# Layer 2 of a graph network: loads of sorted groups one group further ahead, and two blocks of counts no longer stored

## What is computed

```
agg = segment_sum(h[src], dst) / max(cnt, 1)
h   = relu(agg @ W_l + b_l + h @ W_r)                 # twice; the second time is "layer 2"
x   = layernorm(x + h @ W_out + b_out)
...
out    = selu(concat(x[src], edge_attr) @ W1a + b1a) @ W1b + b1b
mean   = segment_sum(out, dst) / max(cnt, 1)
x      = layernorm(x + selu(concat(x, mean, u) @ W2a + b2a) @ W2b + b2b)
```

## Time and profile before

| what | us |
|---|---|
| median of 3 runs | 2593.54 |
| lowest and highest | 2592.89 to 2598.89 |
| the profiled execution | 2589.51 |
| its span in the trace | 2587.8 |
| PE busy | 2099.7 (81%) |
| POOL busy | 1827.1 (71%) |
| DVE busy | 1593.5 (62%) |
| ACT busy | 1000.1 (39%) |

### The profile page before, as it was taken

The page is one execution under the profiler, slowest core; times in us unless marked ns, Lnnn a source line. Parts: engine busy times, 40 slices in busy tenths (PEclk is TensorE's granted clock), DMA queues, the critical chain, the costliest instruction groups (busy, mean ns, idle before and its releaser), DMA issues. The chain is left out here.

```text
span 2587.8 us, 53172 instructions
## 1 busy us (share of the span) xinstructions
PE 2099.7 (81%) x18808; PEld 1547.7 (60%) x18808; DVE 1593.5 (62%) x3209; ACT 1000.1 (39%) x2287; POOL 1827.1 (71%) x1859
## 2 busy tenths in 40 slices
PE   1899999999999999955887788887788788766753
PEld 1555555555555555535766676676676666656653
DVE  6889999994545555454655656565566555543433
ACT  3777787772000000023433334333333333332322
POOL 5535767646777777767777777777777777777775
PEclk9999999998999999966989998889899989986665
DMA  8368778769767878724333333333333333332212
GB/s 295 107 227 247 211 234 259 197 226 251 237 183 222 244 236 243 172 75 118 79 67 77 76 72 69 77 74 74 68 77 69 72 75 76 70 64 55 51 40 45
DMA packets 501618, 350.13 MB, mean 135 GB/s; under 512 B 378596, under 2 KB 452767, under 8 KB 497693
## 3 DMA queue, kind: packets, MB, share of 16 engines
q1 hardware_dynamic: 385571, 274.97, 37.6%
q0 software_dynamic: 54240, 57.27, 10.3%
q10 hardware_dynamic: 61562, 14.60, 3.1%
HBM read 201.07 MB, written 145.49 MB: 134 GB/s over the span
## 5 line engine op out<-in xcount | busy, mean ns | idle before, releaser
L985 POOL DMA_INDIRECT A_sb<-source_terms,src_cur x1132 | 1082.5, 956 | 345.2 <-issue 340.6
L936 POOL DMA_INDIRECT sorted_edges<-pm_row,pm_to x480 | 523.0, 1090 | 178.8 <-issue 137.6
L1870 DVE TENSOR_TENSOR arena<-iota_code,arena 128x2048 f16<-128x2048 f16 (+1 forms) x392 | 438.4, 1186 | 27.5 <-PE cnt_ps L1415 25.4
L1080 ACT ACTIVATE A_sb<-cnt_ps 128x392 f32 (+1 forms) x784 | 383.8, 498 | 125.1 <-PE cnt_ps L1415 84.4
L1544 PE MATMUL agg_ps<-A_sb,arena 128*128 128x448 f16 x1911 | 382.3, 358 | 0.0
L1415 PEld LDWEIGHTS cnt_ps<-arena 128*128 128x128 f16 x3136 | 190.5, 101 | 214.9 <-issue 167.9
L1415 PE MATMUL cnt_ps<-arena 128*128 128x98 f16 x3136 | 281.4, 214 | 31.8 <-ACT A_sb L1080 26.6
L1646 PE MATMUL agg_ps<-A_sb 128*65 128x48 f32 x2264 | 188.6, 245 | 140.9 <-DVE A_sb L2206 140.9
L2193 DVE TENSOR_TENSOR cnt_ps<-cnt_ps,A_sb 128x512 f32<-128x512 f32 (+1 forms) x142 | 98.2, 692 | 315.1 <-DMA A_sb<-source_terms,src_cur 305.5
L1544 PEld LDWEIGHTS agg_ps<-A_sb,arena 128*128 128x128 bf16 x1911 | 187.2, 99 | 167.7 <-issue 9.9
L1228 ACT ACTIVATE A_sb<-cnt_ps 128x512 f32<-128x512 f32 (+1 forms) x142 | 84.3, 594 | 490.4 <-DVE cnt_ps L2193 477.6
(11 more groups left out here) (308 smaller groups left out, 3425.5 us busy)
## 6 DMA issues: line engine op xcount, KB each, us to landing
counts_matrix<-A_sb SPq DMA_DIRECT2D x14, 5488.0 KB, 17.0
A_sb<-counts_matrix SPq DMA_DIRECT2D x12, 5488.0 KB, 18.9
arena<-in_edge_attr_dram SPq DMA_DIRECT2D x93, 256.0 KB
sorted_edges<-zrow SPq DMA_DIRECT2D x12, 1716.0 KB, 12.0
arena<-sorted_edges SPq DMA_DIRECT2D x156, 128.0 KB
A_sb<-source_terms,src_cur POOLq DMA_INDIRECT x1132
overlapping_rows<-A_sb SPq DMA_DIRECT2D x1, 13056.0 KB, 39.4
A_sb<-in_edge_attr_dram SPq DMA_DIRECT2D x48, 256.0 KB
```

Source lines behind the costliest of these rows:

```text
L936: pool.indirect_dma_start(out=sorted_d, out_offset=bass.IndirectOffsetOnAxis(ap=pm_to[:, k, j:j + 1], axis=0), in_=pm_row[:, k, j, :], in_ ...
L985: pool.indirect_dma_start(out=gath[k][:, j * F:(j + 1) * F], out_offset=None, in_=p_d, in_offset=bass.IndirectOffsetOnAxis(ap=src_cur[k][: ...
L1080: act.activation(Asb(half)[:, :, bass.ds((b * BG + k) * GROUP, GROUP)].rearrange("p b (w j) -> p b w j", j=PAIR), cnt_ps[k % 2][:, 0:SUB * ...
L1870: ins = dve.tensor_tensor(hot_rows[:, slots], iota_code[:, 0:n, :].unsqueeze(1).to_broadcast([P, AT_ONCE * SUB // 2, n, 2]), turned[:, bas ...
```

## The change

Three edits.

In stage 1, blocks 12 and 13 of the counts are no longer stored: SP returns ahead of the wait and the store for them, the DRAM tensor has 12 blocks, and SP's wait for all stores counts one less for each half.

In layer 2, ACT issues the third load of a block in another place. `load_group(FIRST[s] + 5)` now stands behind `move_agg2(s)` in every block, where it stood only in four-group blocks. In a three-group block that is group FIRST[s + 1] + 2, and so the load of that group at the start of the next block is dropped. Behind a four-group block, and in block 1, the load at the start of the block stays. Eight loads move: groups 22, 29, 32, 39, 42, 49, 52 and 59.

```
-    A_d = dram("counts_matrix", [NSB, P, SRC_BLOCKS * SBN], FP16)
+    A_d = dram("counts_matrix", [NSB - 2, P, SRC_BLOCKS * SBN], FP16)
...
                     for q in range(s - 1, FROM_SP):
                         load_group(q)
+                if s >= NSB - 2:
+                    return
                 sp.wait_ge(counts_moved, (s + 1) * SB_GROUPS + 2)
...
-            sp.wait_ge(A_stored[0], 16 * PAIRS)
-            sp.wait_ge(A_stored[1], 16 * PAIRS)
+            sp.wait_ge(A_stored[0], 16 * (PAIRS - 1))
+            sp.wait_ge(A_stored[1], 16 * (PAIRS - 1))
...
                     act.activation(hTs[:, :], t_ps[:, 0:SBN], ACT.Copy).then_inc(hT_moved, 1)
-                if s is not None:
+                if s is not None and (s == 1 or LAYER2[s - 1] == 4):
                     load_group(FIRST[s] + 2)
...
                     load_group(FIRST[s] + 4)
                     move_agg2(s)
-                    if LAYER2[s] == 4:
-                        load_group(FIRST[s] + 5)
+                    load_group(FIRST[s] + 5)
```

## The result

| | before | after |
|---|---|---|
| median of 5 runs each, us | 2593.54 | 2576.11 |
| lowest to highest, us | 2590.45 to 2598.89 | 2574.71 to 2582.07 |
| profiled execution, us | 2589.5 | 2574.7 |
| its span, us | 2587.8 | 2573.0 |
| first to last copy of the sums of layer 2, us | 458.3 | 447.1 |

The changed kernel is 17.4 us faster, a ratio of 0.9932 [0.9919, 0.9944]. The forecast was 22.9 us. Between the two profiled executions it is 14.8 us: the gathers start 19.7 sooner, and the stage behind them is 4.9 longer.

What follows compares the result with a forecast made beforehand. The gathers were taken as a fixed-length block, with POOL becoming layer 2's bound. Gathers 20.9 us earlier plus 2 from the stores gave 22.9, so 2593.5 - 22.9, about 2571 us; range 2560 to 2585.

Steps and rivals of the forecast that it cites:

- Rivals 2: Layer 2: early load shares engines with the reload, landing about 716 instead of 719; gain 12 + 2, 2579 us; chance 0.14.
- Rival 1: Layer 2: POOL is no bound, its instructions get shorter, PE's whole side arrives: 29.5 + 2 to 5, 2560 us; chance 0.08.
- rival 3: Layer 2: transfer order makes no difference, or the group is late for its buffer; only the stores' gain left, 2591 us; chance 0.09.
- PE's 29.5 us: Layer 2: PE time lost in four four-group blocks, 7.9 us in one and 21.6 in the other three, stalls and half clock together.
- 20.9 + 2: Gathers start 20.9 us earlier from POOL ending layer 2 sooner, plus 2 us from dropping two stores; 22.9 in sum.
- prediction's own signs of being wrong: Wrong if POOL still waits for DVE, PE's shift ends below 20 us by new lower-clock stalls, or the last stage grows.
- Part 2: Layer 2: POOL becomes the bound, so PE's 29.5 us shrinks to 18.8 on POOL's side; gathers start 20.9 us earlier.
- 25.4 - 6.6 = 18.8 us: Layer 2: POOL's 22 waits for DVE total 25.4 us; less their usual 0.30 us steps, 18.8 can be taken out.
- the landing of 2.5 us: Layer 2: a scatter's buffer comes free 2.5 us after its last scatter ends, a figure taken from a gather.
- the 1.7 us of issues: Layer 2: after group 59's load finds its buffer free at 1072.2, ACT is free 1.7 us of issues later, at 1073.9.
- PE may run up to 23.2 ahead: End of layer 2: ACT's t_ps copy moves at most 19.1 us, plus 4.1 of PE slack; over 18.8, so POOL stays fed.
- rival 4: Layer 2: a moved load whose buffer is late blocks ACT's t_ps copy and PE at eight loads; 2608 us, slower; chance 0.05.

Runs made afterwards that it cites:

- the last run: Changed kernel with the last split of h moved from POOL to DVE and four-group blocks 1, 4, 7, 10: 2571.3 us, ratio 0.9912 to the kernel before.
- short reload: Changed kernel with each layer 2 reload bringing only the first seventh of a counts block: 2571.14 us, ratio 0.9887 to the kernel before.
- the second profile: Changed kernel run again, nothing altered, on the chip of the loads-only and stores-only runs: 2572.52 us, ratio 0.9942 to the kernel before.
- the kernel with the later load: Changed kernel with the remaining start-of-block loads issued behind the copy to h2T: 2580.9 us, ratio 0.992 to the kernel before.
- seven scatters of eight: Changed kernel with groups from 13 on scattered by seven indirect DMAs instead of eight: 2559.52 us, ratio 0.9845 to the kernel before.

## Why the prediction was right, and where it was off

**The mechanism was right.** Four of the eight loads were late behind the reload, and issuing them ahead of it took away DVE's four waits and PE's stalls with their half clock; with the old order and without the stores the waits stand as before (34.5 us). Against its block group 22's load moved by 5.8 us, and DVE had waited 8.20, so being earlier would by itself have left 2.4 us of wait. That the rest is the reload follows from this sum, and the last run points the same way: a load behind the reload, in a four-group block, was late by 7.13 us. No run has the old order with a short reload. Rivals 2 and 3 fall: group 22's destinations are there in time, and PE's scan wait is 0.6 us. Rival 1 falls as well: a scatter takes 985 ns in the mean, not less than 976. On one chip the loads alone bring 13 us where the whole change brings 15. Beside rival 3 the text had set a rule of the Trainium skill (DMA: Bandwidth & Descriptors, Queues, rings and completion order), by which the order of a small and a large transfer on two rows would hardly matter; here it mattered by 33 us of DVE's waits.

**That PE's 29.5 us would not all arrive was right**, and that the gathers would start about when POOL ends too. They start 19.7 us sooner against 20.9 + 2 forecast, but that this is so near is luck: POOL's run gave 10.9 of 18.8, and its start came 8.9 us earlier (630.4 instead of 639.2) where 2 were taken. The prediction's own signs of being wrong came in part: POOL still waits 4.5 us for DVE, PE's last copy moved by 19.8 us, under its 20, with new stalls that lower the clock, and the last stage of that profile grew.

**Part 2, POOL's share, was sized too large.** The step "only 25.4 - 6.6 = 18.8 us can be taken out" was taken as if all would be. 14.3 went, 4.5 stayed. The scatters themselves took 3.4 us more (367.0 to 370.4); a fixed 0.976 us each was the wrong assumption. POOL's run shrank by 10.9 us.

**The step that failed is the landing of 2.5 us, with the 1.7 us of issues behind it.** The landing was taken from a gather in the last stage, where no reload runs. Beside a reload a scatter's buffer comes free 7 to 14 us after its last instruction, as the lags of groups 36, 40, 46 and 49 show. The issues of one load were priced at 1.7 us; in block 10 they take 6.9 (968.42 to 975.33), and in block 7 of the second profile 12.0 (861.14 to 873.15), nearly all of it one stuck issue. "PE may run up to 23.2 ahead" rested on both. In fact PE met held loads in blocks 6 and 10, and they gave back 39.5 + 42.5 - 66.0 = 16 us. That is the mechanism of rival 4, at two blocks and not at eight loads, and one of the two was a load that had not moved (group 36, held at the copy to h2T). PE's side of layer 2 is 11.2 us shorter instead of 29.5. The iota shows it: forecast without a wait, it waits 2.15 us for PE's source terms.

**Part 3 was sized too small.** 2 us were taken, 6.0 [3.1, 8.8] measured, just outside the bound of 5, though the interval reaches inside it. PE's wait for the rows of x is gone, as forecast, but the half clock that follows it in the earlier trace rows was left out of the 2. The 20 us from just ahead of the same matmul (622.63 and 616.13), before and then in the changed kernel:

```profile
622.60:642.60 20.00, 19.97 (x93) 12.50 (x94) 4.07 (x13) 1.38 (x3) 10.71 (x12) 0.74 1.13 244
```

```profile
615.50:635.50 20.00, 19.33 (x106) 11.15 (x104) 5.40 (x19) 2.24 (x5) 13.86 (x15) 0.91 0.97 204
```

The granted clock is 0.91 instead of 0.74, which over 20 us is 20 x 0.17 = 3.4 us of full-speed work; with the wait of 1.70 that makes 5.1. POOL waits 2.60 us for ACT's h instead of 6.86. That these two make up the 6.0 is an estimate. This error and the one before it lean against each other, and the sum came out nearer than its terms.

**The last stage did not have the same length.** It differs between executions of the same code. In ten profiles of kernels with the same last stage a gather's mean is 956 or 957 ns in seven, with 1445.8 to 1447.5 us from the iota on, and 961 or 962 in three, with 1451.1 to 1452.8. The changed kernel has 961 in the first profile and 956 in the two others on comparable chips, so the 4.9 us are no effect of the change. What decides between the two lengths stays open. It may well be part of what the short reload's time left unexplained, since that kernel's profile has the short length and that of the kernel it is compared with the long one.

## What to carry to other kernels

A small load issued behind a large one came late here: issue it ahead, and look what it waits for. In this ring of buffers the gain of a removed stall was capped by the idle time of the next engine in the ring. Price every term of such a cap under the traffic that runs at that moment; a landing time from a quiet stage was 5 to 12 us short here. A load that waits for a buffer and stands ahead of a copy turns a late buffer into a stall of whoever needs the copy.

## What the runs showed of the hardware

- The end of an indirect scatter is not the release of its buffer. ACT's waiting load follows the last scatter's end by 1.2 us with no reload under way, and by 11 to 14 us in the middle of one of 5488 KB, often until the reload's landing (19.1 us in the median). With reloads of a seventh it is 1.2 to 4.6.
- A DMA issue can itself be stuck beside a reload: 5.51 us at 969.82 in the changed kernel, 10.79 at 870.42 in the kernel with the later load, against 0.45 to 0.68 at 687 ahead of it. With reloads of a seventh none takes over 2 us.
- Between the first and last copy of layer 2, PE's half clock followed each stall of 2.3 to 7.3 us and was absent where it had none (granted clock 1.00 over the 430.0 us with seven scatters of eight), so a stall of 4.8 us cost 7.9.
- Gathers take 956 or 961 ns in the mean, by execution, which is 5 us over 1132 of them.
- One chip ran the kernel before and four others in about 3500 us; the changed kernel had the same busy times of POOL and DVE there, and 1060.2 us of idle time between gathers.
